# A decay scan moved from TensorE to shifted additions on VectorE, with the shifts done by DMA

## The chip, the cores and the metric

The kernel runs on one core of one Trainium2 chip. The metric is the device time of one execution in microseconds. Before the change the median of three runs is 786.25 us (785.98 to 786.61).

## The reference, cut to what matters

Two blocks work on x of 16 batches x 512 positions x 512 features in float32.

```python
x = x + rmsnorm(layernorm(x), g_res) @ W_in.T + b_in + depool_out   # first block
h_patch = rmsnorm(ctx_2048, g_init)                   # 16 x 512 patches x 1024, the first 512 are used
a = exp(dt * A)                                       # one constant, the same for every row
s[i] = a * s[i-1] + u[i]                              # the scan, over the patches of a batch
depool_out[i] = s[plug[i]]                            # rows picked by a running count of marks
y = layernorm(x)                                      # second block
xr, xk = mixes of y and y moved by one position       # mu_r, mu_k
x = x + sigmoid(xr @ W_r.T) * (relu(xk @ W_k.T)**2 @ W_v.T)
```

The decay `a` is about 0.001, so that after 13 powers nothing is left above the smallest float32 number. For nearly all batches only the first 128 patches are picked; batches with more are called far.

## The kernel before, in words

A batch goes through four stages, and one iteration of the loop works on three batches at once: `b` in the second block, `nxt` = b + 1 in the first block's projection, `new` = b + 2 in its preparation. `batches` (L62) writes iterations -1 and 0 out, runs 1 to 12 as a hardware loop of four rounds of three, and writes the last three out. Every engine has its own instruction list in an order written out by hand, and semaphores hold them together (`reached`, L54, waits for a count that belongs to a batch).

Matrix products are exact to float32 by three products each (`product`, L484 to L486): high by high, high by low, low by high part. ScalarE makes the high part (`copy`, L704), VectorE the low part by subtraction (`low`, L894). TensorE in an iteration: project `nxt` (48 matmuls), gate product of `b` (48), key product (48), value products of tiles 0 and 1 (24), the scan of `new` (3, `scan`, L506), a look at a table whether `new` is far (`far`, L512), value products of tiles 2 and 3 (24), and the transposes of `nxt` (16, `turn`, L578). The scan is a product with a 128 x 128 matrix of the powers of the decay, into bank 3. The fourth group of transposes writes bank 3 too and waits for the semaphores s_copied and far_over of `new` (L584 and L585).

VectorE in an iteration: mixing of `b` with the additions to `nxt` between (L989, L1019), statistics of `nxt` (L1025) and of `new` (L923), normalisation of `nxt` (L1038), four low parts of the keys of `b` (`ka_low`, L894) with two subtractions for xt and the scan's input u (L947) between, u's low part, gating of tiles 0 and 1 (L1044), the scan's output `scanned` (bank 3 plus the bias, L905), the look at the table (L269, L270), far_over, the outputs of tiles 0 and 1 (L919), gating and outputs of tiles 2 and 3.

ScalarE, among the rest, squares ctx, copies xt's high part, squares the keys, copies u's high part, then issues the store of `scanned` to `s_rows` in DRAM (L742), and copies the transposes out (`turned_out`). GpSimd adds rows of `s_rows` to x by four indirect DMAs (L426) once the store has landed. SP waits for these, then loads xt (L285), x (L282) and ctx (L288) of the next `new`, and stores the outputs (L335), all in the order of its list. The lines that fix that order:

```python
rows_added(sp, new.plus(-1))
reached(sp, xt_lo_ready, new.plus(-1), 2, 2); load_xt(new)
reached(sp, out_ready, b.plus(-1), T, T);     load_x(new)
reached(sp, far_over, new.plus(-1), 1, 1);    load_ctx(new)
```

Of the kernel before, what the change touches and what calls it, by code (L numbers as in the profile page):

```python
# [17 lines left out]
P = 128  # L18
# [54 lines left out]

def decay_powers():

    one = np.float32(1.0)
    dt = np.float32(-math.log(-math.expm1(float(np.float32(-EPSILON)))))
    a = np.float32(math.exp(-float(dt)))
    powers = [one]
    while powers[-1] * a > np.finfo(np.float32).tiny:  # L80
        powers.append(powers[-1] * a)
    return [float(p) for p in powers]


def build(nc, x, x_turned, ctx, patch_lens, w_in, b_in, columns, g_init, w_r, w_k, w_v, out):
# [10 lines left out]
    powers = decay_powers()  # L96
    input_gain = math.exp(-EPSILON)

    with ExitStack() as stack:
# [62 lines left out]
        patch_now = sb("patch_now", [P, T], U32)  # L162

# [17 lines left out]
        def f32(ap):  # L181
# [31 lines left out]
            "u_ready u_hi_ready u_lo_ready s_done s_copied s_stored patch_picked")  # L213
        dep_added = [sem(f"dep_added{t}") for t in range(T)]
# [62 lines left out]
        def _(sp):  # L277
# [37 lines left out]

            def iteration(b):
                new = b.plus(2)
                if new.exists(B) and not is_first(new, 1):

                    rows_added(sp, new.plus(-1))  # L320
                    reached(sp, xt_lo_ready, new.plus(-1), 2, 2)
                    load_xt(new)


                    reached(sp, out_ready, b.plus(-1), T, T)
                    if is_first(new, 2):
                        sp.wait_ge(w_lo_ready[WK], C)
                    load_x(new)

                    reached(sp, far_over, new.plus(-1), 1, 1)  # L330
                    load_ctx(new)
                if b.exists(B):
                    for t in range(T):
                        reached(sp, out_ready, b, T, t + 1)
                        sp.dma_start(out_rows[b.number(), :, t, :], gate[:, t, :]).then_inc(stored[t], 16)  # L335
# [145 lines left out]
        def _(pe):  # L481
# [30 lines left out]
            def far(b):  # L512

                n = far_count(pe, b)
                with pe.If(n[0] > 0):
                    for c in range(1, T):
                        done = n[1] * (T - 1) + c
                        if c > 1:
                            pe.wait_ge(far_copied, done - 1)
                        else:  # L520
                            reached(pe, s_copied, b, 1, 1)

                        product(scan_bank(b)[:, :], decay_hi[:, 1, :], decay_lo[:, 1, :], u_hi[:, :], u_lo[:, :],
                                True, False).then_inc(far_carried, 1)
                        pe.wait_ge(far_u_lo, done)
                        product(scan_bank(b)[:, :], decay_hi[:, 0, :], decay_lo[:, 0, :], u_hi[:, :], u_lo[:, :],
                                False, True).then_inc(far_s, 1)
# [50 lines left out]
            def turn(b):  # L578

                for t in range(T):  # L580
                    reached(pe, yn_ready, b, T, t + 1)
                    if b.plus(-1).exists(B):
                        reached(pe, relu_ready, b.plus(-1), C, t + 1)
                    if t == SCAN and b.plus(1).exists(B) and not is_first(b):  # L584
                        reached(pe, s_copied, b.plus(1), 1, 1)  # L585
                        reached(pe, far_over, b.plus(1), 1, 1)
                    for c in range(C):
                        last = nc.tensor.transpose(first_bank(b, t)[:, tile(c)], normed[:, t, c * P:(c + 1) * P],  # L588
                                                   ident[:, :])
                    last.then_inc(yn_turned, 1)  # L590

            def iteration(b):
# [21 lines left out]
                if new.exists(B):  # L614
                    scan(new)
                    far(new)
# [85 lines left out]
        def _(act):  # L702
# [106 lines left out]
            def iteration(b):  # L809
# [18 lines left out]
                if is_first(b):  # L828
                    squares(b)
                    u_high(new)  # L830
# [14 lines left out]
                elif new.exists(B):  # L845
                    if not is_first(b):
                        u_high(new)
# [33 lines left out]
        def _(dve):  # L881
# [61 lines left out]
            def scan_input(b):  # L943

                reached(dve, rs_c_done, b, 1, 1)
                reached(dve, u_lo_ready, b.plus(-1), 1, 1)
                nc.vector.scalar_tensor_tensor(u[:, :], ctx_rows[:, 0:D], rs_c[:, :], g_ctx[:, :],  # L947
                                               ALU.mult, ALU.mult).then_inc(u_ready, 1)

            def far(b):  # L950

                n = far_count(dve, b)
                with dve.If(n[0] > 0):
                    for c in range(1, T):
# [19 lines left out]
                        dve.wait_ge(far_u_hi, done)  # L974
# [76 lines left out]
            def iteration(b):  # L1051
# [32 lines left out]
                if is_first(b):  # L1084

                    ka_low(b, 0)
# [6 lines left out]
                    u_low(new)  # L1093
                    norm_b(nxt)
                    gating(b, 0)
                    gating(b, 1)
                    x_lo(new, 0)
                    x_lo(new, 1)
                    scan_out(new)
                    far(new)  # L1100
                    dve.sem_inc(far_over, 1)
                    add_out(b, 0)
                    add_out(b, 1)
# [5 lines left out]
                if new.exists(B):  # L1109
                    stats_a(new)  # L1110
                    stats_c(new)
                if nxt.exists(B):
                    norm_b(nxt)
                for m in range(C):
                    if b.exists(B):
                        ka_low(b, m)
                    if new.exists(B):
                        if m in (1, 2):
                            x_lo(new, m - 1)
                        if m == 2:  # L1120
                            scan_input(new)
                if is_last(nxt):
                    mixing(nxt, 0, C)
                if new.exists(B):
                    u_low(new)
# [3 lines left out]
                if new.exists(B):  # L1129
                    scan_out(new)  # L1130
                    far(new)
                    dve.sem_inc(far_over, 1)
                if b.exists(B):
                    add_out(b, 0)
                    add_out(b, 1)
# [138 lines left out]
```

## Time and profile before

| | |
|---|---|
| median of three runs | 786.25 us |
| the profiled execution | 788.05 us, its span 786.5 us |
| granted clock of TensorE, mean | 0.986 |
| busy: TensorE, weight loads, VectorE, ScalarE, GpSimd | 756.9, 624.1, 553.8, 413.3, 173.4 us |
| DMA | 85.73 MB, mean 109 GB/s |

A row of a timeline begins with the start in us from the span's start and the duration; a group of like instructions stands on one row. PE is TensorE, DVE VectorE, ACT ScalarE, POOL GpSimd, SP the engine that issues most DMAs; a q behind a name is that engine's own instruction sequencer. The text in square brackets is the idle time of the engine ahead of the row, and what ended it; "issue" is a wait for nothing that the profile shows. Matmuls overlap: they start 0.227 us apart though each lasts 0.39.

### The profile page before, as it was taken

The page shows a single profiled execution, that of the slowest core. Times are in us where ns is not written, and L with a number is a line of the kernel's source. Part 1 is how long each engine was busy: PE and PEld are TensorE (multiplying, and loading weights), DVE is VectorE, ACT ScalarE, POOL GpSimd, SP SyncE. Part 2 cuts the span into 40 slices and gives each one's busy share as a digit, 9 for nine tenths or more (in the row PEclk, how much of TensorE's full clock was granted, in tenths as well). Part 3 has the DMA queues.
Part 4 walks back from the last instruction along what each step waited for, and adds up shares of the span by engine and source line. Part 5 has one row for each costly group of instructions (what it writes and reads, how often), then busy time and mean ns, then how long its engine had stood idle before and what let it go on. Part 6 is the DMA issues. An engine that isn't in the chain of part 4 may idle for free.

```text
span 786.5 us, 11081 instructions
## 1 busy us (share of the span) xinstructions
PE 756.9 (96%) x3462; PEld 624.1 (79%) x3463; DVE 553.8 (70%) x1005; ACT 413.3 (53%) x681; POOL 173.4 (22%) x175
## 2 busy tenths in 40 slices
PE   7669899999999999999999999999999999999997
PEld 4457688888888888888888888888888888888876
DVE  4678797685866868586686858667685867667452
ACT  3317755454654645466464546656454665544760
POOL 7244131311213131121313112131311213130000
PEclk9879999999999999999999999999999999999999
DMA  7476153441706244170624417062441706231011
GB/s 256 150 188 166 60 124 132 112 143 47 209 2 167 88 110 144 46 208 0 156 98 109 144 43 211 0 166 88 108 146 41 212 0 160 94 102 20 1 54 54
DMA packets 42765, 85.73 MB, mean 109 GB/s; under 512 B 3536, under 2 KB 3536, under 8 KB 42704
## 3 DMA queue, kind: packets, MB, share of 16 engines
q1 hardware_dynamic: 30624, 63.71, 21.7%
q0 software_dynamic: 9216, 16.78, 13.5%
q10 hardware_dynamic: 2880, 4.76, 1.7%
q14 instruction: 31, 0.25, 0.1%
q8 instruction: 14, 0.23, 0.1%
HBM read 64.26 MB, written 21.76 MB: 109 GB/s over the span
## 4 chain that ended last, share of the span: by engine, by line
PE 85%; DVE 4%; POOL 4%; issue 2%; ACT 2%; DMA 1%; DVEq 0%; POOLq 0%; ACTq 0%
PE bank L484 27%; PE bank L486 27%; PE bank L485 27%; PE bank L588 3%; POOL ring L426 2%; DMA s_rows<-scanned 1%; POOL decay L363 1%; DVE xk_lo L894 1%; DVE scratch L989 0%; DVE ring L1019 0%; DVE gate L1044 0%; ACT scratch L794 0%; POOL rs_a L389 0%; DVE bn_a L923 0%; DVE bn_b L1025 0%
## 5 line engine op out<-in xcount | busy, mean ns | idle before, releaser
L426 POOL DMA_INDIRECT ring<-s_rows,patch_now x60 | 99.4, 1656 | 245.8 <-DMA s_rows<-scanned 214.6
L894 DVE TENSOR_TENSOR xr_lo<-scratch,xr_hi 128x512 fp32r<-128x512 f32 x124 | 85.6, 690 | 68.9 <-ACT xr_hi L704 68.4
L989 DVE SCALAR_TENSOR_TENSOR scratch<-turned,cols,scratch 128x512 f32<-128x512 f32 x128 | 94.6, 749 | 34.4 <-ACT scratch L749 15.0
L484 PE MATMUL bank<-wi_hi,xt_hi 128*128 128x512 f32 x256 | 104.0, 406 | 5.1 <-DVE xt_lo L894 5.1
L704 ACT ACTIVATE turned<-bank 128x512 f32<-128x512 f32 x64 | 33.4, 604 | 143.3 <-PE bank L588 114.7
L484 PE MATMUL bank<-xk_hi,wk_hi 128*128 128x512 f32 x256 | 99.9, 390 | 2.2 <-DVE xk_lo L894 2.2
L485 PE MATMUL bank<-wi_lo,xt_hi 128*128 128x512 f32 x256 | 101.8, 398 | 0.0
L486 PE MATMUL bank<-wi_hi,xt_lo 128*128 128x512 f32 x256 | 101.5, 396 | 0.0
L484 PE MATMUL bank<-wr_hi,xr_hi 128*128 128x512 f32 x256 | 99.7, 389 | 0.8 <-DVE xr_lo L894 0.8
L486 PE MATMUL bank<-xk_hi,wk_lo 128*128 128x512 f32 x256 | 99.6, 389 | 0.0
L485 PE MATMUL bank<-xk_lo,wk_hi 128*128 128x512 f32 x256 | 99.6, 389 | 0.0
L486 PE MATMUL bank<-wr_hi,xr_lo 128*128 128x512 f32 x256 | 99.6, 389 | 0.0
L485 PE MATMUL bank<-wr_lo,xr_hi 128*128 128x512 f32 x256 | 99.6, 389 | 0.0
L484 PE MATMUL bank<-wv_hi,xr_hi 128*128 128x512 f32 x240 | 94.0, 392 | 2.7 <-DVE xr_lo L894 2.7
L486 PE MATMUL bank<-wv_hi,xr_lo 128*128 128x512 f32 x240 | 93.4, 389 | 0.0
L485 PE MATMUL bank<-wv_lo,xr_hi 128*128 128x512 f32 x240 | 93.4, 389 | 0.0
L749 ACT ACTIVATE scratch<-turned,cols 128x512 f32<-128x512 f32 x128 | 89.5, 711 | 0.5
L704 ACT ACTIVATE xr_hi<-scratch 128x512 fp32r<-128x512 f32 x124 | 77.9, 628 | 20.4 <-DVE scratch L989 17.7
L781 ACT ACTIVATE gate<-bank 128x512 f32<-128x512 f32 x64 | 37.5, 595 | 83.3 <-PE bank L486 83.3
L1044 DVE TENSOR_TENSOR gate<-bank,gate 128x512 f32<-128x512 f32 x64 | 43.6, 688 | 53.2 <-PE bank L486 51.2
L395 POOL TENSOR_TENSOR rs_b<-v_b,half 128x4 f32<-128x4 f32 x16 | 16.5, 1034 | 230.5 <-DVE v_b L1031 230.5
L704 ACT ACTIVATE xk_hi<-scratch 128x512 fp32r<-128x512 f32 x64 | 40.4, 632 | 47.6 <-DVE scratch L989 46.8
(131 smaller groups left out, 1283.5 us busy)
## 6 DMA issues: line engine op xcount, KB each, us to landing
ring<-in_x SPq DMA_DIRECT2D x16, 1024.0 KB, 7.4
out<-gate SPq DMA_DIRECT2D x64, 256.0 KB
xt<-in_x_turned SPq DMA_DIRECT2D x15, 1024.0 KB, 5.2
ctx_rows<-in_ctx SPq DMA_DIRECT2D x16, 512.0 KB, 8.0
s_rows<-scanned ACTq DMA_DIRECT2D x16, 256.0 KB, 2.0
gate<-in_L_xattn_W_in SPq DMA_DIRECT2D x4, 256.0 KB, 3.4
xt<-in_x_turned SPq DMA_DIRECT2D x2, 512.0 KB, 6.3
turned<-in_L_ffn_W_r SPq DMA_DIRECT2D x1, 1024.0 KB, 7.8
```

Source lines behind the costliest of these rows:

```text
L395: nc.gpsimd.tensor_tensor(rs_b[:, :, 0], v_b[:, :, 0], half[:, :], ALU.pow).then_inc(rs_b_done, 1)
L426: pool.indirect_dma_start(ring[b.slot][:, t, :], None, s_rows[:, :], bass.IndirectOffsetOnAxis(ap=rows, axis=0), compute_op=ALU.add).then_ ...
L484: nc.tensor.matmul(where, lhs_hi, rhs_hi, start=start, stop=False)
L485: nc.tensor.matmul(where, lhs_hi, rhs_lo, start=False, stop=False)
L486: return nc.tensor.matmul(where, lhs_lo, rhs_hi, start=False, stop=stop)
L588: last = nc.tensor.transpose(first_bank(b, t)[:, tile(c)], normed[:, t, c * P:(c + 1) * P], ident[:, :])
L704: return nc.scalar.activation(to, of, ACT.Copy)
L749: nc.scalar.activation(scratch[:, i % 2, :], turned[:, c, 0:S], ACT.Copy, scale=cols[:, 3 + which, c:c + 1]).then_inc(carried, 1)
L781: nc.scalar.activation(gate[:, t, :], bank[4 + t][:, :], ACT.Sigmoid).then_inc(gate_ready, 1)
L894: return nc.vector.tensor_tensor(to, whole, high, ALU.subtract)
L989: nc.vector.scalar_tensor_tensor(scratch[:, 2 + i % 2, :], turned[:, c, 1:S + 1], cols[:, 1 + which, c:c + 1], scratch[:, i % 2, :], ALU.m ...
L1044: nc.vector.tensor_tensor(gate[:, t, :], bank[4 + t][:, :], gate[:, t, :], ALU.mult).then_inc(gated, 1)
```

## The change

From batch 2 on there is no scan on TensorE, and no high and low part of u, except in a far batch, where VectorE makes both. Instead VectorE makes four steps `scanned = decay**k * earlier + scanned` with k = 8, 4, 2, 1 (the first adds to u), and ahead of each step SP moves `scanned` (or u) down by k partitions into the new tile `earlier`, by two DMAs: 112 rows, and the rest of 8, 12, 14 or 15. The first rows of `earlier` are zeroed once per batch. After step 3 the bias is added by an instruction of its own. In the loop the input of the scan is made ahead of the low parts of the keys; step 0 takes its place behind the third low part, step 1 follows the fourth, step 2 follows gating 1, and the outputs of tiles 0 and 1 come between steps 2 and 3. The look at the table and far_over follow the bias. TensorE's fourth group of transposes waits for far_over alone. SP loads ctx first, then x, then xt, then issues the shifts, then the output stores. The diff, cut to its core (the semaphore and tile declarations are left out):

```diff
+
+
+def shift_steps(powers):
+
+    return [(k, powers[k] if k < len(powers) else 0.0) for k in (8, 4, 2, 1)]
...
+    steps_of_scan = shift_steps(powers)
+    STEPS, MOST = len(steps_of_scan), P - 16
+    assert len(powers) <= 2 ** STEPS
...
+            def shift_scan(b):
+
+                since = b.plus(-2)
+                for n, (k, _) in enumerate(steps_of_scan):
+                    if n == 0:
+
+                        reached(sp, u_ready, b, 1, 1)
+                    else:
+
+                        reached(sp, earlier_added, since, STEPS, n)
+                    of = scanned if n else u
+                    sp.dma_start(earlier[k:k + MOST, :], of[0:MOST, :]).then_inc(earlier_loaded, 16)
+                    sp.dma_start(earlier[k + MOST:P, :], of[MOST:P - k, :]).then_inc(rest_loaded, 16)
+
             def iteration(b):
                 new = b.plus(2)
                 if new.exists(B) and not is_first(new, 1):
 
+                    reached(sp, far_over, new.plus(-1), 1, 1)
                     rows_added(sp, new.plus(-1))
-                    reached(sp, xt_lo_ready, new.plus(-1), 2, 2)
-                    load_xt(new)
-
+                    load_ctx(new)
 
                     reached(sp, out_ready, b.plus(-1), T, T)
                     if is_first(new, 2):
                         sp.wait_ge(w_lo_ready[WK], C)
                     load_x(new)
 
-                    reached(sp, far_over, new.plus(-1), 1, 1)
-                    load_ctx(new)
+                    reached(sp, xt_lo_ready, new.plus(-1), 2, 2)
+                    load_xt(new)
+                    shift_scan(new)
...
-                            reached(pe, s_copied, b, 1, 1)
+                            if b.fixed and b.number() < 2:
+                                reached(pe, s_copied, b, 1, 1)
+                            pe.wait_ge(far_u_lo, n[1] * T + 1)
 
                         product(scan_bank(b)[:, :], decay_hi[:, 1, :], decay_lo[:, 1, :], u_hi[:, :], u_lo[:, :],
                                 True, False).then_inc(far_carried, 1)
-                        pe.wait_ge(far_u_lo, done)
+                        pe.wait_ge(far_u_lo, n[1] * T + c + 1)
...
                     if t == SCAN and b.plus(1).exists(B) and not is_first(b):
-                        reached(pe, s_copied, b.plus(1), 1, 1)
                         reached(pe, far_over, b.plus(1), 1, 1)
...
                 if new.exists(B):
-                    scan(new)
                     far(new)
...
-                    u_high(new)
...
                 elif new.exists(B):
-                    if not is_first(b):
-                        u_high(new)
                     store_scan(new)
...
                 reached(dve, rs_c_done, b, 1, 1)
-                reached(dve, u_lo_ready, b.plus(-1), 1, 1)
+                if b.fixed and b.number() < 3:
+                    reached(dve, u_lo_ready, b.plus(-1), 1, 1)
+                else:
+
+                    reached(dve, earlier_added, b.plus(-3), STEPS, STEPS)
                 nc.vector.scalar_tensor_tensor(u[:, :], ctx_rows[:, 0:D], rs_c[:, :], g_ctx[:, :],
                                                ALU.mult, ALU.mult).then_inc(u_ready, 1)
 
+            def clear_head(b):
+
+
+                reached(dve, earlier_added, b.plus(-2), STEPS, 0)
+                nc.vector.memset(earlier[0:steps_of_scan[0][0], :], 0.0).then_inc(head_zeroed, 1)
+
+            def scan_step(b, n):
+
+                since = b.plus(-2)
+                reached(dve, earlier_loaded, since, 16 * STEPS, 16 * (n + 1))
+                reached(dve, rest_loaded, since, 16 * STEPS, 16 * (n + 1))
+                if n == 0:
+                    reached(dve, head_zeroed, since, 1, 1)
+
+                    reached(dve, s_stored, b, 16, 0)
+                    reached(dve, u_ready, b, 1, 1)
+                else:
+                    reached(dve, earlier_added, since, STEPS, n)
+                nc.vector.scalar_tensor_tensor(scanned[:, :], earlier[:, :], steps_of_scan[n][1], (scanned if n else u)[:, :],
+                                               ALU.mult, ALU.add).then_inc(earlier_added, 1)
+
+            def add_bias(b):
+
+                reached(dve, earlier_added, b.plus(-2), STEPS, STEPS)
+                nc.vector.tensor_tensor(scanned[:, :], scanned[:, :], bias[:, :], ALU.add).then_inc(s_copied, 1)
...
                 with dve.If(n[0] > 0):
+                    if b.fixed and b.number() < 2:
+
+                        reached(dve, s_done, b, 1, 1)
+                    nc.vector.tensor_copy(u_hi[:, :], u[:, :]).then_inc(far_u_hi, 1)
+                    dve.wait_ge(far_u_hi, n[1] * T + 1)
+                    low(u_lo[:, :], u[:, :], f32(u_hi[:, :])).then_inc(far_u_lo, 1)
+                    dve.wait_ge(far_u_lo, n[1] * T + 1)
...
 
+                    clear_head(new)
                     ka_low(b, 0)
                     stats_c(new)
                     ka_low(b, 1)
@@ -1090,49 +1149,57 @@
                     ka_low(b, 2)
                     stats_a(new)
                     ka_low(b, 3)
-                    u_low(new)
+                    scan_step(new, 0)
                     norm_b(nxt)
                     gating(b, 0)
                     gating(b, 1)
+                    scan_step(new, 1)
                     x_lo(new, 0)
                     x_lo(new, 1)
-                    scan_out(new)
+                    scan_step(new, 2)
+                    add_out(b, 0)
+                    add_out(b, 1)
+                    scan_step(new, 3)
+                    add_bias(new)
                     far(new)
                     dve.sem_inc(far_over, 1)
-                    add_out(b, 0)
-                    add_out(b, 1)
...
                 if new.exists(B):
+                    clear_head(new)
                     stats_a(new)
                     stats_c(new)
                 if nxt.exists(B):
                     norm_b(nxt)
+                if new.exists(B):
+                    scan_input(new)
                 for m in range(C):
                     if b.exists(B):
                         ka_low(b, m)
                     if new.exists(B):
                         if m in (1, 2):
                             x_lo(new, m - 1)
-                        if m == 2:
-                            scan_input(new)
+                        if m in (2, 3):
+                            scan_step(new, m - 2)
                 if is_last(nxt):
                     mixing(nxt, 0, C)
-                if new.exists(B):
-                    u_low(new)
                 if b.exists(B):
                     gating(b, 0)
                     gating(b, 1)
                 if new.exists(B):
-                    scan_out(new)
+                    scan_step(new, 2)
+                if b.exists(B):
+                    add_out(b, 0)
+                    add_out(b, 1)
+                if new.exists(B):
+                    scan_step(new, 3)
+                    add_bias(new)
                     far(new)
                     dve.sem_inc(far_over, 1)
                 if b.exists(B):
-                    add_out(b, 0)
-                    add_out(b, 1)
```

## Rows read from the trace of the kernel before

**Rows 1.** The page's first section: busy time, share of the span, instructions.
```profile
PE 756.9 (96%) x3462; PEld 624.1 (79%) x3463; DVE 553.8 (70%) x1005; ACT 413.3 (53%) x681; POOL 173.4 (22%) x175
```

**Rows 2.** The waits of TensorE's array from 60 us on: total, times, longest.
```profile
PE bank L484 <- DVE xr_lo L894: 3.5, 5, 0.9
PE bank L484 <- DVE xk_lo L894: 2.2, 2, 1.2
```

**Rows 3.** Timeline of TensorE: start, duration, what; one iteration and its ends.
```profile
332.92 1.91 PE L588 MATMUL bank<-ident,normed 128*128 128x128 f32 x16
...
372.76 0.39 PE L484 MATMUL bank<-u_hi,decay_hi 128*128 128x512 f32 x1
...
373.44 0.39 PE L484 MATMUL bank<-wv_hi,xr_hi 128*128 128x512 f32 x1
...
378.89 1.91 PE L588 MATMUL bank<-ident,normed 128*128 128x128 f32 x16
380.55 0.48 PE L484 MATMUL bank<-wi_hi,xt_hi 128*128 128x512 f32 x1
```

**Rows 4.** Timeline of VectorE in the same iteration.
```profile
352.96 0.38 DVE L1029 BATCH_NORM_AGGREGATE mv_b<-bn_b 128x2 f32<-128x6 f32 x4 [0.16 <-DVE bn_b L1025]
...
353.45 2.46 DVE L923 BATCH_NORM_STATS2 bn_a<-ring 128x6 f32<-128x512 f32 x4
...
362.02 0.69 DVE L894 TENSOR_TENSOR xr_lo<-scratch,xr_hi 128x512 fp32r<-128x512 f32 x1 [1.71 <-ACT xr_hi L704]
...
368.51 0.74 DVE L947 SCALAR_TENSOR_TENSOR u<-ctx_rows,rs_c,g_ctx 128x512 f32<-128x512 f32 x1
...
372.28 1.37 DVE L1044 TENSOR_TENSOR gate<-bank,gate 128x512 f32<-128x512 f32 x2 [1.50 <-PE bank L486]
373.74 0.69 DVE L905 TENSOR_TENSOR scanned<-bank,bias 128x512 f32<-128x512 f32 x1
```

**Rows 5.** Wait behind the table look: all, then the last one, outside the loop.
```profile
DVE gate L919 <- issue: 17.0, 13, 1.5
697.00 1.29 DVE L919 TENSOR_TENSOR gate<-gate,ring 128x512 f32<-128x512 f32 x2 [0.89 <-issue]
```

**Rows 6.** The page's DMA issues: KB each, median us from issue to landing.
```profile
ring<-in_x SPq DMA_DIRECT2D x16, 1024.0 KB, 7.4
...
ctx_rows<-in_ctx SPq DMA_DIRECT2D x16, 512.0 KB, 8.0
s_rows<-scanned ACTq DMA_DIRECT2D x16, 256.0 KB, 2.0
gate<-in_L_xattn_W_in SPq DMA_DIRECT2D x4, 256.0 KB, 3.4
```

**Rows 7.** Stretches behind the issue at 374.46; the last columns are DMA share, GB/s.
```profile
375.00:375.30 0.30, 0.30 (x3) 0.23 (x2) 0.00 (x0) 0.00 (x0) 0.00 (x0) 1.00 0.02 7
...
375.90:376.20 0.30, 0.30 (x3) 0.22 (x2) 0.30 (x2) 0.00 (x0) 0.00 (x0) 1.00 0.22 75
```

**Rows 8.** Timelines of ScalarE, GpSimd and SP: issues of DMAs.
```profile
374.46 0.33 ACTq L742 DMA_DIRECT2D s_rows<-scanned  x1
377.27 1.64 POOL L426 DMA_INDIRECT ring<-s_rows,patch_now  x1 [16.84 <-DMA s_rows<-scanned]
343.42 0.41 SPq L285 DMA_DIRECT2D xt<-in_x_turned  x1
```

**Rows 9.** Sequencer of TensorE, L67 (the loop's jump): ns min/median/max, starts.
```profile
L67 PEldq COMPARE_BRANCH  x1: 208/208/208, 378.5 to 378.5; - x1
```

**Rows 10.** Iteration 0: timelines of VectorE and TensorE.
```profile
97.64 1.27 DVE L1044 TENSOR_TENSOR gate<-bank,gate 128x512 f32<-128x512 f32 x2
98.84 2.34 DVE L894 TENSOR_TENSOR xt_lo<-xt,xt_hi 128x1024 fp32r<-128x1024 f32 x2
...
104.73 0.47 PE L484 MATMUL bank<-wi_hi,xt_hi 128*128 128x512 f32 x1
```

**Rows 11.** A stretch of iteration 0: length, PE busy, ..., granted clock, DMA share, GB/s.
```profile
90.00:100.00 10.00, 8.45 (x35) 6.19 (x36) 9.35 (x21) 4.99 (x8) 1.94 (x2) 1.00 0.00 1
```

More of the change, by code:

```diff
@@ L162, in build @@
         patch_now = sb("patch_now", [P, T], U32)
+        earlier = sb("earlier", [P, D])
         def part(row, start, shape, dt):
@@ L213, in build @@
             "u_ready u_hi_ready u_lo_ready s_done s_copied s_stored patch_picked")
+        head_zeroed, earlier_loaded, rest_loaded, earlier_added = sems("head_zeroed earlier_loaded rest_loaded earlier_added")
         dep_added = [sem(f"dep_added{t}") for t in range(T)]
@@ L973, in far @@
                         nc.vector.tensor_copy(u_hi[:, :], u[:, :]).then_inc(far_u_hi, 1)
-                        dve.wait_ge(far_u_hi, done)
+                        dve.wait_ge(far_u_hi, n[1] * T + c + 1)
                         low(u_lo[:, :], u[:, :], f32(u_hi[:, :])).then_inc(far_u_lo, 1)
```

## The prediction

> **What bounds the kernel now.** I read the page's first section, the waits of TensorE, then the timelines of TensorE and VectorE over one round of the loop. TensorE is busy 96% of the span [rows 1]. After 60 us its array waits seven times for anything, 5.7 us in all [rows 2], so its own work is the bound. One iteration (one batch through the stages) lasts 45.97 us, from the transposes at 332.92 to those at 378.89 [rows 3]. The three matmuls of the scan stand at 372.76, and the next product follows at 373.44: they cost 0.68 us of a full array [rows 3]. VectorE has holes: 1.71 us before the first low part of the keys, 1.50 us before the gating, and another behind the scan's output [rows 4, 5].
>
> **What the change takes from TensorE.** Batches 2 to 15 lose their scan: 14 x 0.68 = 9.5 us if nothing else moves. ScalarE loses a copy, VectorE a subtraction and the read of the bank.
>
> **What it adds: a chain of four steps.** Step 0 of VectorE takes the place that the input of the scan had, at 368.51 for 0.74 us [rows 4]. The input moves into the 1.71 us hole ahead of 362.02, behind the statistics of 353.45 and the normalisation; its first shift then has some 7 us, more than it needs. The 8-row memset is small and ahead of a wait too. From step 0 on each step needs the one before it moved through a DMA pair issued by SP, and nothing hides that. Let G be the time from the end of one step to the start of the next. No row shows a transfer from SBUF to SBUF, so I bound it:
> - Nearest row: the 256 KB store of the scan, from SBUF, lands 2.0 us after its issue [rows 6]. Issued at 374.46, its packets run from about 375.3 to 376.1 [rows 7, 8]: 0.84 us before the first, some 0.75 of moving, some 0.4 to the landing. 112 of 128 rows save 1/8 of the moving: 1.9.
> - The second transfer is issued 0.4 us behind the first (0.33 us an issue on ACT [rows 8], and a gap). Its one row per engine stands behind seven of the first; it lands at about 2.0.
> - Waking SP costs 0.03 (store issued at 374.46, addition ended at 374.43 [rows 4, 8]); two further waits and their register operations in front of the next step cost about 0.1.
>
> So G is 1.9 at the least; at most it is that of the 256 KB loads from DRAM, 3.4 us and 0.2 [rows 6]. I take 2.15, near the store, which also reads SBUF.
>
> Then, in the frame of [rows 4]:
> - step 0: 368.51 to 369.26. The last low part of the keys, right behind it, keeps its place.
> - step 1: 371.41 to 372.16. Gating 0 and 1 keep theirs (372.28, for 1.37).
> - step 2: 374.31 to 375.06; two output additions fit behind it.
> - step 3: 377.21 to 377.96.
> - bias: from 378.12 (a dependent instruction starts 0.16 later [rows 4]), 4.4 us after the old scan output at 373.74.
> - far_over: behind that output comes the look at the table of far batches. Its mean gap is 17.0/13 = 1.31 us [rows 5], and with 0.69 for the addition 2.00 from its start; the increment is some 0.12 before the next instruction. So far_over rises at 380.00.
>
> **Who waits for that.** The fourth group of transposes waits for far_over (L578 to 586), unchanged in the code; before, the rise at about 375.4 was 4.8 us early. The sixteen take 1.66 us, 378.89 to 380.55 [rows 3], so without the scan the fourth group would start at 378.21 + 1.25 = 379.46. It now waits to 380.00, 0.54 us. And TensorE's sequencer, ahead of the array until now, stands at that wait. Behind it come the wait itself (0.08), eight instructions (0.25), every third iteration the loop's jump (0.208 and its registers, 0.43 in all, 0.14 on average [rows 9]) and 0.40 of waits and registers up to the projection's first matmul (in the timeline of the sequencer from 380.2, the matmul at 380.55 [rows 3]): 0.87; the small terms are estimates from instructions of 20 to 50 ns around [rows 9]. The projection starts at 380.87 where it started at 380.55. An iteration is longer by 0.32 us, not shorter by 0.68. In formula: 3G - 6.13.
>
> **The sum.** Twelve iterations of the loop: 12 x 0.32 = +3.8. The last with a scan stands outside the loop: its look takes 0.89 + 0.69 = 1.58 instead of 2.00 [rows 5] and there is no jump: 0.32 - 0.56 = -0.2. Iteration 0 is different: there VectorE works without holes and its sequencer had the look done in advance. Step 0 is over before 96, and the gatings, 97.64 to 98.9, come before step 1 (98.9 to 99.6), two subtractions (2.34 us [rows 10]) before step 2, at 101.85 to 102.5; step 3 starts at 104.65 and ends at 105.4, the bias starts at 105.55, far_over rises 1.47 later at 107.0, and the projection starts at about 107.95 where it started at 104.73 [rows 10]: +3.2. Together +6.9 on the profiled execution's 788.05, so 794.9. That execution is 1.8 above the median of the runs; against 786.25 the forecast is 793.1.
>
> **What stays covered.** The bias comes 4.1 us later relative to the next projection (378.12 - 380.87 against 373.74 - 380.55), and so do the store, the indirect additions (POOL at 377.27 [rows 8]) and the loads that wait for them (343.42 becomes 347.5). x is now second, behind ctx of half its size. Before it stood behind xt and landed 0.5 + 7.4 = 7.9 us after the first issue [rows 6]; 1.3 less is 6.6, at 354.1. The statistics of 353.45 slip by 0.65 into the hole ahead of 358. xt, last, lands at about 356.6 (before, the last of the three landed 8.0 us after its own issue [rows 6], 1.1 behind the first), and ScalarE reads it from 358.2. The indirect additions had landed by 343.4, when SP issued; 4.1 us later each is still ahead of the addition that reads it, the second by only 0.3. SP's output stores stand behind the shifts, whose last is issued at 375.1, ahead of the first output. The clock was 1.00, the 2.4 GHz level, also where the array was busy 8.45 of 10 us [rows 11]; waits of half a microsecond don't touch it.
>
> The Trainium skill, SBUF — State Buffer, section The DMA setup-cost knee, says that every transfer pays a roughly fixed 2 us beside its bytes. With the 0.6 us of moving in these rows a shift would land after 2.6 and G would be about 2.7. The store of 256 KB lands after 2.0 in all, moving included [rows 6], so this trace disagrees for that transfer; no row settles it for SBUF to SBUF.
>
> **Rivals.** The time moves by 41 us per microsecond of G (12 x 3, 3 and 2 in the two iterations outside), so no change lies at G = 1.98.
> - Hidden (faster): the shift lands before 1.95, since an SBUF target might confirm sooner than DRAM. From G = 1.82 down the fourth group waits no longer in the loop: 13 x -0.68 + 2.6 for iteration 0 = -6.2, about 780. For it: only 0.17 us separate me from no change. Against it: 0.84 before the first packet is on the sending side, and two issues in a row add to it.
> - Slow shifts: at 2.7, because seven rows an engine run unevenly, or the confirmation is slow: 0.55 x 41 = +22.5 on my forecast, 815. For it: loads of the same size took 3.4, and 2.7 is a third of the way from my value to the upper bound.
>   The Trainium skill's fixed 2 us (the section above) would give about this G.
> - The late loads: if the indirect additions slow down beside the later stores so that x comes 3 us later still, the hole ahead of 362.02 is used up and the low parts that TensorE needs come about 1 us late, 13 x 1 = +13: 806. Against it: the margins above.
> - The change doesn't take TensorE's work away: not so by the diff; the scan call is gone from the iteration.
>
> **Chances.** Forecast (G 2.02 to 2.4): 0.53, by itself 787.8 to 803.5. At or about no change (G 1.94 to 2.02): 0.13. Hidden or partly hidden: 0.22. Slow shifts 0.08. Late loads 0.04. This gives faster 0.22, within 0.2% (1.6 us, about what can be told from no change) 0.13, slower 0.65. The range, G 1.87 to 2.45: 782 to 805.
>
> **What would show it.** Three scan matmuls fewer per batch, and TensorE with a new wait for VectorE or for nothing named ahead of a transpose or of a projection, some 0.5 to 1 us each iteration; an iteration of 46.3 us; idle time of VectorE ahead of steps 1, 2 and 3, of 1.2, 0.7 and 0.9 us, ended by a DMA from `scanned`; a landing of about 2.0 us for `earlier<-scanned`; iteration 0 longer by 3 us. It is wrong if the landing is under 1.8 us, if the fourth group of transposes starts without a gap, or if new waits stand at the low parts of the keys.

## The result and the profile after

The changed kernel took 827.31 us (median of 4 runs, 826.14 to 831.60); the kernel before took 786.43 us beside it (4 runs, 785.98 to 786.74). The ratio is 1.053, interval 1.049 to 1.057: slower by 5.3%. The forecast was 793.1 with a range of 782 to 805. The sign was right, the size was not, and the range missed by 22 us. The profiled execution took 831.60 us (span 830.0), 43.6 more than the profiled execution before.

The page's first section of the changed kernel answers to [rows 1]:

```profile
PE 764.9 (92%) x3420; PEld 626.6 (75%) x3421; DVE 586.5 (71%) x1061; ACT 406.9 (49%) x667; POOL 189.1 (23%) x175
```

There are 42 matmuls fewer, 14 x 3, so the work left TensorE as planned. Its busy time nevertheless grew by 8 us and its share fell from 96% to 92%. The waits of TensorE's array from 60 us on answer to [rows 2] (total, times, longest):

```profile
PE bank L613 <- DVEq L1201: 32.5, 13, 3.0
PE bank L613 <- DVEq L1165: 4.3, 1, 4.3
PE bank L508 <- DVE xr_lo L915: 2.7, 4, 0.8
PE bank L508 <- DVE xk_lo L915: 2.2, 2, 1.2
```

The last two were there before. The first two are new: the fourth group of transposes (L613) waits for far_over, which VectorE's sequencer raises, 36.8 us in 14 batches. One row of the page's groups, and three of its DMA issues, name what VectorE itself waits for:

```profile
L993 DVE SCALAR_TENSOR_TENSOR scanned<-earlier,scanned 128x512 f32<-128x512 f32 x42 | 29.1, 692 | 76.0 <-DMA earlier<-scanned 76.0
...
earlier<-scanned SPq DMA_DIRECT2D x42, 224.0 KB, 2.7
...
s_rows<-scanned ACTq DMA_DIRECT2D x16, 256.0 KB, 2.0
earlier<-u SPq DMA_DIRECT2D x14, 224.0 KB, 2.7
```

The 42 dependent steps idle 1.8 us each for a transfer that lands 2.7 us after its issue. Here is one iteration; the timeline of VectorE, with the square brackets giving the idle time ahead of a row, answers to [rows 4]:

```profile
392.50 0.68 DVE L993 SCALAR_TENSOR_TENSOR scanned<-earlier,u 128x512 f32<-128x512 f32 x1
393.48 0.69 DVE L915 TENSOR_TENSOR xr_lo<-scratch,xr_hi 128x512 fp32r<-128x512 f32 x1 [0.29 <-ACT xr_hi L728]
396.04 0.69 DVE L993 SCALAR_TENSOR_TENSOR scanned<-earlier,scanned 128x512 f32<-128x512 f32 x1 [1.86 <-DMA earlier<-scanned]
396.65 1.28 DVE L1102 TENSOR_TENSOR gate<-bank,gate 128x512 f32<-128x512 f32 x2
399.62 0.69 DVE L993 SCALAR_TENSOR_TENSOR scanned<-earlier,scanned 128x512 f32<-128x512 f32 x1 [1.69 <-DMA earlier<-scanned]
400.23 1.29 DVE L940 TENSOR_TENSOR gate<-gate,ring 128x512 f32<-128x512 f32 x2
403.21 0.69 DVE L993 SCALAR_TENSOR_TENSOR scanned<-earlier,scanned 128x512 f32<-128x512 f32 x1 [1.69 <-DMA earlier<-scanned]
403.94 0.69 DVE L999 TENSOR_TENSOR scanned<-scanned,bias 128x512 f32<-128x512 f32 x1
406.11 1.29 DVE L1102 TENSOR_TENSOR gate<-bank,gate 128x512 f32<-128x512 f32 x2 [1.48 <-issue]
```

From the end of one step to the start of the next, G, it is 2.86, 2.89 and 2.90 us (396.04 less 392.50 and 0.68, and so on). The order of the rows is the one forecast; the gaps aren't. The issues of the second shift, in the timeline of SP, and the end of the iteration on TensorE, which answers to [rows 3]:

```profile
393.22 0.53 SPq L337 DMA_DIRECT2D earlier<-scanned  x1
393.79 0.77 SPq L338 DMA_DIRECT2D earlier<-scanned  x1
```

```profile
402.20 1.47 PE L613 MATMUL bank<-ident,normed 128*128 128x128 f32 x12
406.00 1.11 PE L613 MATMUL bank<-ident,normed 128*128 128x128 f32 x4 [2.32 <-DVEq L1201]
406.76 0.77 PE L508 MATMUL bank<-wi_hi,xt_hi 128*128 128x512 f32 x1
407.33 0.63 PE L509 MATMUL bank<-wi_lo,xt_hi 128*128 128x512 f32 x1
```

TensorE finishes twelve transposes, stops 2.32 us, does four, and then its matmuls start 0.43 us apart, not 0.227. The granted clock in the next view says why: the first line is the stretch behind the stop, the second all of the run behind 72 us, and the second fence the same of the kernel before. The columns are the stretch, its length, the busy time of PE, PEld, DVE, ACT and POOL, the granted clock, the DMA share and GB/s:

```profile
406.00:409.00 3.00, 3.00 (x9) 2.56 (x10) 2.49 (x4) 2.57 (x5) 1.53 (x1) 0.50 0.07 27
72.00:830.00 758.00, 712.57 (x3184) 587.04 (x3182) 540.30 (x964) 379.72 (x621) 153.56 (x113) 0.98 0.40 114
```

```profile
72.00:786.00 714.00, 705.14 (x3226) 584.75 (x3224) 507.65 (x908) 386.21 (x635) 137.09 (x113) 1.00 0.34 101
```

Behind the stop TensorE runs at 0.50 of its clock, the 1.2 GHz level, and over all of the run behind 72 us the mean is 0.98; before, it was 1.00. The clock fell behind six of the fourteen stops (those of 4.3, 3.0, 2.9, 3.0, 2.3 and 3.0 us), each time for 3.4 or 6.8 us. It didn't fall behind any of the last six, from 500 us on, though they were of 2.0 to 3.0 us too. What tells the one kind from the other wasn't found.

### The profile page after: what moved, and what is told of

Same layout as the page of the kernel before. It is cut to its first block, busy times and chain, and to the rows that moved or that the text cites. A ratio compares the mean times of both kernels' runs of the same rounds, so it can differ in the third digit from the quotient of the medians.

```text
span 830.0 us, 11255 instructions
## 1 busy us (share of the span) xinstructions
PE 764.9 (92%) x3420; PEld 626.6 (75%) x3421; DVE 586.5 (71%) x1061; ACT 406.9 (49%) x667; POOL 189.1 (23%) x175
## 4 chain that ended last, share of the span: by engine, by line
PE 57%; DMA 15%; DVE 11%; ACT 5%; issue 5%; POOL 4%; DVEq 2%; SPq 1%; POOLq 0%; ACTq 0%
PE bank L508 19%; PE bank L509 19%; PE bank L510 19%; DMA earlier<-scanned 13%; DVE scanned L993 5%; DVE xt_lo L915 2%; POOL ring L450 2%; DMA s_rows<-scanned 2%; ACT scratch L818 1%; PE bank L613 1%; POOL decay L387 1%; ACT scratch L816 1%; ACT xr_hi L728 1%; DVEq L280 1%; SPq L337 1%
## 5 line engine op out<-in xcount | busy, mean ns | idle before, releaser
L450 POOL DMA_INDIRECT ring<-s_rows,patch_now x60 | 110.2, 1837 | 332.3 <-DMA s_rows<-scanned 294.3
L508 PE MATMUL bank<-wi_hi,xt_hi 128*128 128x512 f32 x256 | 108.9, 425 | 5.4 <-DVE xt_lo L915 5.4
L509 PE MATMUL bank<-wi_lo,xt_hi 128*128 128x512 f32 x256 | 106.2, 415 | 0.0
L510 PE MATMUL bank<-wi_hi,xt_lo 128*128 128x512 f32 x256 | 105.7, 413 | 0.0
L993 DVE SCALAR_TENSOR_TENSOR scanned<-earlier,scanned 128x512 f32<-128x512 f32 x42 | 29.1, 692 | 76.0 <-DMA earlier<-scanned 76.0
L613 PE MATMUL bank<-ident,normed 128*128 128x128 f32 x256 | 36.9, 292 | 43.0 <-DVEq L1201 32.5
L613 PEld LDWEIGHTS bank<-ident,normed 128*128 128x128 f32 x256 | 31.1, 150 | 48.6 <-DVEq L1201 32.7
```

The costliest lines, as they stand in the source:

```text
L450: pool.indirect_dma_start(ring[b.slot][:, t, :], None, s_rows[:, :], bass.IndirectOffsetOnAxis(ap=rows, axis=0), compute_op=ALU.add).then_ ...
L508: nc.tensor.matmul(where, lhs_hi, rhs_hi, start=start, stop=False)
L509: nc.tensor.matmul(where, lhs_hi, rhs_lo, start=False, stop=False)
L510: return nc.tensor.matmul(where, lhs_lo, rhs_hi, start=False, stop=stop)
L993: nc.vector.scalar_tensor_tensor(scanned[:, :], earlier[:, :], steps_of_scan[n][1], (scanned if n else u)[:, :], ALU.mult, ALU.add).then_i ...
```

## The experiments

The kernel before, run beside all of these, took 786.5 to 787.2 us. What the runs had to decide: is the loss the chain of dependent shifts (theory), or the other things that the change touches; what sets G; what the clock costs; and which waits tie the chain to TensorE.

**One transfer instead of four.**

```diff
 in shift_scan, for n in 0..3:
-    of = scanned if n else u
-    (both transfers)
+    if n == 0: (both transfers, from u)
 in scan_step:
-    wait for the transfers of step n
+    wait for the transfers of step 0
```

> Leaves out the transfers of steps 1 to 3 (every step adds the first shift again; the scan's numbers are wrong), all four additions, the bias and the order stay. Theory A (the chain of transfers holds TensorE back): without the three gaps the bias starts about 400.3 in the frame where it started at 403.9, far_over rises before the fourth group is due, the period falls to 45.3 us, and the time to 777 to 780. Rival B (VectorE's added work, SP's new order or the late loads cost it): 800 or more. Rival C (half of the loss is the clock for a cause of its own): about 790.

Measured: 781.28 us, ratio 0.992 (0.990 to 0.995), within 2 us of the theory. From one first transpose to the next it takes 45.29 us in twelve of the iterations: 45.97 less exactly the 0.68 us of the scan's three products. Everything else of the change is in this kernel (four additions, the moved input, the memset, the new order of loads, one shift a batch), and all of it is hidden in the loop. The exception is iteration 0, where one period is 49.41: VectorE comes late there by its own work, and TensorE still stops 2.3 us for far_over. The whole loss against the kernel before goes with the three dependent transfers.

**What a shift costs: its shape and its number.**

```diff
 e2_112_alone
-    earlier[k+112:128] <- of[112:128-k]
 e4_112_in_place
-    (both transfers)
+    earlier[16:128] <- of[16:128]
 e3_128_in_place
-    (both transfers)
+    earlier[0:128] <- of[0:128]
```

> Leaves out the second transfer of each shift (the last rows of the moved tile stay old). If the 112-row transfer sets the gap: it still lands after 2.7 us, the gap is 2.75 instead of 2.88, time 820 to 824. If the second transfer and its issue set it: the gap falls to 2.2, time below 800.

> Each shift is one transfer of rows 16 to 127 to the same rows: 112 rows, not moved. If the count of 112 makes it slow: issue 0.53, landing 2.6 to 2.7, time 815 to 822, as with 112 rows moved. If the move to other partitions makes it slow: landing 2.0, time 784 to 790.

> Each shift is one transfer of all 128 rows to the same rows, so nothing is shifted. If a transfer within SBUF costs what the store did and only the shape of this one is dear: issue 0.33, landing 2.0, gap 2.15, the wait of the fourth group some 0.1 to 0.2 us, time 784 to 790, about the forecast. If the target SBUF is slower by itself: landing 2.7, time 820 to 824.

Measured: 812.78 (ratio 1.032, 1.027 to 1.038), 811.35 (1.031, 1.028 to 1.034) and 802.71 us (1.020, 1.016 to 1.024). The views of all instructions that touch `earlier` give the durations of the issue (ns, min/median/max) and the landings. First the changed kernel, then e2_112_alone, then e3_128_in_place:

```profile
L337 SPq DMA_DIRECT2D earlier<-scanned x42: 517/532/551, 96.0 to 740.0; - x42
L338 SPq DMA_DIRECT2D earlier<-scanned x42: 766/818/1252, 96.5 to 740.5; - x42
...
DMA to landing us min/median/max: 2.6/2.7/3.3
```

```profile
L337 SPq DMA_DIRECT2D earlier<-scanned x42: 511/512/517, 94.8 to 719.7; - x42
...
  DMA earlier<-scanned: 63.8, 41
...
DMA to landing us min/median/max: 2.6/2.6/3.1
```

```profile
L337 SPq DMA_DIRECT2D earlier<-scanned x42: 464/465/471, 94.3 to 710.4; - x42
...
  DMA earlier<-scanned: 52.5, 40
...
DMA to landing us min/median/max: 2.3/2.3/3.8
```

The median G of the 42 gaps is 2.89 in the changed kernel, 2.69 without the short transfer, 2.66 with 112 rows that are copied onto their own rows, 2.36 with 128 rows. So the displacement of the rows costs 0.03 at most; the short transfer costs 0.20; and 112 rows cost 0.3 more than 128, though they are fewer bytes. The packets in the traces say where the 0.3 lies (medians): the first starts 1.13 us behind the issue with 128 rows and 1.18 with 112, they run for 0.79 and 1.07 us, and from the end of the last to the landing it takes 0.39 and 0.36. In one transfer of 112 rows that I counted through, six packets or fewer are in flight in the last 0.3 us, where 16 are before. Why they are spread so isn't shown. Each of the three lies between the two results that I had set against each other. None makes the loss vanish: at the 2.36 of one full transfer the kernel is still 2% slower. The wait of TensorE's array for far_over falls with G as it should, from 36.8 us in all to 25.1, 24.4 and 16.1.

**The clock by itself.**

```diff
 in the turn of the fourth group, ahead of the wait for far_over:
+    for _ in range(10): matmul into the free bank, result not used
```

> The changed kernel with ten more products on TensorE (results not used) into a bank that is free, placed right ahead of the fourth group of transposes, so that the array works on through most of its stop for far_over. The chain of shifts and additions is untouched, so far_over comes no earlier. Theory A (TensorE's array idles 2.3 to 4.5 us there, the granted clock falls to 1.2 GHz for a stretch of 3.4 us behind it in 7 to 9 of 14 iterations, and these stretches cost some 10 us in all): no half-speed stretch after the first 72 us of the span, granted clock back at 0.983 or more, periods of 47.5 to 48.0 us (48.6 where an instruction fetch delays a shift) instead of 49.4 to 51.3, about 814 to 818 us. Rival B (the clock's fall has another cause, or costs nothing because VectorE's and ScalarE's work sets the pace behind it): 826 us or more.

Measured: 819.91 us (ratio 1.042, 1.040 to 1.045), 7.4 less than the changed kernel, with ten products more a batch. The stretch behind 72 us in this kernel:

```profile
72.00:817.00 745.00, 731.08 (x3316) 602.08 (x3314) 539.25 (x962) 378.99 (x621) 151.34 (x113) 1.00 0.41 116
```

Behind iteration 0 the periods are 47.6 to 48.6 us where five of the changed kernel's were 49.4 to 51.3. One stretch at half clock was left against my expectation, at 108.1 us, behind the 2.2 us that remained of iteration 0's stop. The idle array costs twice: for the stop itself, and for the half clock behind it. The second part is 7.4 us of the medians. The result lies 2 us above what I expected, where I had priced the half clock at some 10 us in all: too much by a quarter.

**Which waits tie the chain to TensorE.**

```diff
 e6_over_early, VectorE
+    far(new); far_over        ahead of scan step 1
-    far(new); far_over        behind the bias
 e7_store_on_sp
-    ScalarE: store_scan(new)  ahead of turned_out
+    SP: the same store, behind the fourth shift
 e8_both
     both edits
```

> The changed kernel with far (the sum of the middle entries, with the look at the register and far_over behind it) moved ahead of the scan's first addition on VectorE, so that far_over doesn't wait for the four additions. Theory A (two things hang on the chain's end: far_over, and behind it ScalarE, which issues the store of the scanned rows and only then turns the transposed rows; the store waits for the bias addition): TensorE stops for ScalarE's turned rows almost as long as it did for far_over, about 822 to 828 us. Rival B (only far_over holds TensorE): the scan is hidden, 776 to 782 us.

> The changed kernel with the store of the scanned rows issued by SyncE behind the shifts, not by ScalarE; far_over stays behind the four additions. Theory A (far_over binds by itself, ScalarE's part lies just behind it): 822 to 828 us, no gain. Rival B (only ScalarE's wait at the store holds the work up): 776 to 782 us.

> Both edits together: far ahead of the scan on VectorE, and the store of the scanned rows issued by SyncE. Theory A (far_over and the store are the only two that hang on the chain within the stretch that bounds): the chain of four shifts runs beside TensorE's other work, TensorE's stop is gone, no half-speed stretch behind it, periods near 45.3 us (46.0 less the 0.68 us of the scan's products), 776 to 783 us, faster than the kernel before. Rival B (a third thing hangs on it: VectorE's additions of the scan come between the normed rows and their turned copies, or the loads issued behind the shifts, or the indirect additions that wait for the store, come late and stop TensorE elsewhere): 790 to 815 us.

Measured: 821.82 (ratio 1.045, 1.043 to 1.047), 829.40 (1.054, 1.052 to 1.057) and 788.56 us (1.002, 1.001 to 1.004). The waits of TensorE's array from 60 us on, in e6_over_early, then in e7_store_on_sp:

```profile
PE bank L508 <- ACT turned L728: 34.9, 14, 4.8
```

```profile
PE bank L616 <- DVEq L1202: 32.7, 13, 3.2
PE bank L616 <- DVEq L1166: 4.8, 1, 4.8
```

Each edit alone removes one of two waits that end almost together (undisturbed periods are 47.4 us in e6_over_early and 47.5 in e7_store_on_sp and the changed kernel), and the other takes over whole: 34.9 us for the turned rows of ScalarE, which stands at its issue of the scan's store until the bias is added, or 37.5 for far_over. Only together do they set TensorE free of the chain. Theory A of both held to within 1.4 us, but e8_both did not reach its 776 to 783, nor quite its rival's 790 to 815. Behind iteration 0 its periods are 45.3 to 47.7 us. Three views of it show what comes late next: the waits of all engines, those of TensorE's array from 60 us on, and the timeline of SP:

```profile
ACT xt_hi L731 <- DMA xt<-in_x_turned: 30.1, 14, 4.1
```

```profile
PE bank L511 <- DVE xr_lo L916: 6.6, 11, 0.8
```

```profile
351.36 0.38 SPq L295 DMA_DIRECT2D xt<-in_x_turned  x1
```

xt is issued 18.7 us behind the first transposes (332.70 in this iteration); before it was 10.5 [rows 3, 8]. The store of the scan still comes at the end of the chain, the indirect additions behind the store, and SP's loads wait for these.

> The kernel of e8_both (far ahead of the scan, the store of the scanned rows by SyncE) with one more edit: SyncE issues ctx and xt ahead of its wait for the added rows, not behind it; only x stays behind that wait. In e8_both xt was issued 19 us after the first group of transposes (before: 10.5 us) and ScalarE's conversion of it started 2.5 to 2.8 us later than before, while some periods were 46.1 to 47.7 us instead of 45.3. Theory A (the late xt is what kept e8_both from its gain): conversions back at 25.3 us, all periods 45.3 us, 777 to 783 us. Rival B (VectorE's order, with far ahead and three additions of the chain held by transfers, makes the low parts late): no change from e8_both, 785 to 791 us.

```diff
 SP, in iteration:
     wait far_over; load_ctx(new)
+    wait xt_lo_ready; load_xt(new)
     rows_added(new.plus(-1)); ... load_x(new)
-    wait xt_lo_ready; load_xt(new)
```

Measured: 797.31 us (ratio 1.014, 1.011 to 1.016), worse than e8_both. ScalarE's conversion came 25.3 to 26.0 us behind the first transposes in all but one iteration of the loop (before 25.3, in e8_both 26.0 to 29.7), nearly as theory A has it, but VectorE now waited for the indirect additions (first fence, the waits of all engines), and TensorE more for the low parts (second, its array from 60 us on):

```profile
DVE ring L1077 <- DMA ring<-s_rows,patch_now: 41.2, 22, 4.2
```

```profile
PE bank L510 <- DVE xr_lo L915: 13.1, 19, 1.5
```

In e8_both VectorE's wait was 7.6 us, 9 times, and TensorE's 6.6, 11 times. The 1 MB of xt now moves while the additions do, and these are slower or later; how much of that is contention was not separated. My theory was wrong here, and so was its rival, which forecast no change. That the late xt is what kept e8_both from its gain is therefore read from the traces and not shown: the one run that took the lateness away brought another wait.

**A shorter chain.**

```diff
 def shift_steps(powers):
-    for k in (8, 4, 2, 1)
+    for k in (2, 1)             e10_two_steps
+    for k in (4, 2, 1)          e11_three_steps
 VectorE: the calls of scan_step for the steps that are gone
```

> The changed kernel with two steps of the scan instead of four (shifts by 2 and 1; what the shifts by 8 and 4 add carries factors of the decay's eighth and fourth power, 1e-24 and 1e-12, under the rounding of float32). Two gaps of 2.88 us and two additions of 0.69 us leave the chain: 7.1 us, more than TensorE's stop of 2.3 to 3.3 us. Theory A (the chain's length against the room of about 6.65 us is all that matters): no stop at far_over, no half-speed stretch, each of 14 periods shorter by the 0.68 us of TensorE's products, 776 to 781 us, faster than before. Rival B (the order of SyncE's loads or the wait of SyncE within the chain makes something else late): 784 to 792 us, as with e8_both.

> The changed kernel with three steps of the scan (shifts by 4, 2 and 1), the third addition in the place of the fourth. The chain is shorter by one gap and one addition, 3.57 us, where TensorE's stop costs 2.2 us in most periods and 3.3 us in those in which an instruction fetch delays a shift. Theory A (threshold: two gaps fit, three don't): periods of 45.3 us but for the first (47 to 48), 779 to 784 us. Rival B (the cost falls in proportion to the number of transfers: two thirds of what four steps cost over e1_first_shift_only): 810 to 814 us.

Measured: 779.05 us with two steps (ratio 0.990, 0.988 to 0.992) and 784.53 with three (0.997, 0.996 to 0.998); both are faster than before. In e10_two_steps, the timeline of VectorE, then of TensorE:

```profile
364.12 0.68 DVE L992 SCALAR_TENSOR_TENSOR scanned<-earlier,u 128x512 f32<-128x512 f32 x1
...
367.73 0.69 DVE L992 SCALAR_TENSOR_TENSOR scanned<-earlier,scanned 128x512 f32<-128x512 f32 x1 [1.95 <-DMA earlier<-scanned]
...
370.74 0.68 DVE L998 TENSOR_TENSOR scanned<-scanned,bias 128x512 f32<-128x512 f32 x1
```

```profile
373.82 1.91 PE L612 MATMUL bank<-ident,normed 128*128 128x128 f32 x16
375.48 0.48 PE L507 MATMUL bank<-wi_hi,xt_hi 128*128 128x512 f32 x1
```

The gap is as long as ever (2.93 here, 2.98 in the median), but there is only one, and it fits into the room ahead of the fourth group; the sixteen transposes are one group again and the period is 45.3 us from iteration 1 on. With three steps the periods are 45.3 to 46.6, and 47.4 in iteration 0. The loss is a threshold, not a price per transfer: two thirds of the loss was the rival's forecast (810 to 814).

## Why the prediction was wrong, step by step

- **Taken from TensorE, 14 x 0.68: right.** e1_first_shift_only shows the period of 45.29.
- **What was costed at nothing on VectorE and SP: right in the loop.** The moved input, the memset, ctx ahead of x and xt, and the wait for the added rows cost nothing in e1_first_shift_only behind iteration 0. In the changed kernel VectorE waits 6.8 us in all for x, and TensorE's waits for low parts are no more than before.
- **G: wrong, and the step that failed.** I read 1.9 for the transfer out of the store of 256 KB and 2.15 for G. The median is 2.89, the mean over the 42 gaps 3.01. The bounds (1.9 to 3.6) held it, but the nearest row was not near: each term was too small but the last. The first packet starts 1.19 us behind the issue, not 0.84; the packets of 112 rows run for 1.1 us, not 7/8 of 0.75 (e2_112_alone); the second transfer adds 0.20, not 0.1. From the last packet to the landing it is 0.36, near the 0.4 that I took. With the formula's own 41 us per microsecond, 0.86 of mean is 35 us.
- **The frame around the chain: right in kind, some 0.65 us too long.** From step 3 to the bias it takes 0.73, not 0.91; far_over rises 1.63 to 1.98 behind the bias (mean 1.75), not 1.88; and the restart behind it, forecast at 0.87 with its share of the loop's jump, is 0.48 without the jump and some 0.2 more with it: the group starts 0.07 behind far_over and the projection 0.41 behind the group. With 2.88 for G this gives 3 x 2.88 - 6.13 - 0.18 - 0.25 - 0.39 = +1.69 for a look of 1.63 and no jump; the trace has 47.53 less 45.97, +1.56. Over the twelve iterations of the loop this took back some 8 us.
- **Iteration 0 and the last: right in working.** In the forecast's own frame, from one projection's start to the next, iteration 0 gained 4.4 us (109.14 for 104.73) where +3.2 was forecast. Two of its gaps hang on G, as the forecast had it, and 0.73 more in each of them makes 4.7. The last gained 2.2 for -0.2, of which 2.6 by its gaps of 2.85, 3.36 and 2.87, less the frame.
- **The clock: a term put at nothing, and the second step that failed.** "Waits of half a microsecond don't touch it" is borne out by e3_128_in_place, where nine stops of 0.4 to 0.8 us behind 256 us left the clock at 1.00. But it didn't answer the question. With the true G the stops were 2.0 to 4.3 us, and the clock fell behind six of the fourteen. That is 7.4 us of the median. Of the profiled execution it is some 10 us: the twelve iterations of the loop took 36.9 us more than before in the changed kernel and 26.9 more in e5_filled. (The two profiled executions differ by 12.5 us, but 1.8 of that lie ahead of 57 us, where no chain has begun.) A term that is zero at one value of G isn't zero at the end of the range; the price of 41 us per microsecond left it out.
- **The sum with what was measured:** 6.9 + 35 (G) - 8 (frame) + 10 (clock) = 44, against 43.6 in the profiled execution.
- **Rivals.** "Slow shifts" was what happened, with 0.08 of the chances, and for one of its two reasons: the rows of a transfer of 112 do run unevenly, while the confirmation isn't slow (0.36). Its G of 2.7 is the landing time itself, and its 815 is what the shape without the short transfer gave (812.78). "Hidden" failed on the chip, and "Late loads" stayed covered. The price of G was right to within the frame: e3_128_in_place against the changed kernel moves 24.6 us for 0.52 of mean G, of which 0.52 x 41 = 21; the clock fell less often there too, behind two stops.

The forecast's other weakness was in the width: a quantity without a row, counted three times in series in each of 14 batches, was given 0.3 to either side.

## What to carry to other kernels

A transfer in a chain of dependent steps costs its whole time from issue to landing. Before such a chain is given in exchange for 0.68 us of a busy engine, look at what room it has (here some 6.5 us for three gaps: three of 8.65 in all, in the iteration that ends at 358 us, brought the fourth group 2.1 us late) and count a gap at some 2.9 us. Shorten the chain before moving its ends, for everything that hangs on its end has to move with it: here two waits, each hiding the other, and a store with the loads behind it. And price a stop of the array with its after-effect: of fourteen stops of 2.0 to 4.3 us here, six were followed by 3.4 or 6.8 us at half clock.

## What the runs showed of the hardware that I had not expected

- A transfer of 112 rows from SBUF to SBUF lands later (2.6 us) than one of 128 rows (2.3), and its issue takes 0.51 against 0.465 us; in place or displaced makes a difference of 0.03 at most. The issue of the short one takes 0.82 with 12 to 15 rows and 0.72 with 8.
- The same 256 KB land in 2.0 us in DRAM (the store) and in 2.3 in SBUF. The Trainium skill, DMA: Bandwidth & Descriptors, section Latency and other measured facts, holds that the receipt from the target memory dominates the fixed cost and that HBM is the slowest target; these two rows stand against it. The issuing engine isn't the reason: in e7_store_on_sp, where SP issues the store, it lands in 2.0 too. Nor is the receipt: from the end of the last packet to the landing it is 0.35 us in DRAM and 0.39 in SBUF, and the rest of the difference lies ahead of the first packet (0.84 against 1.13 behind the issue). The Trainium skill, SBUF — State Buffer, section The DMA setup-cost knee, advises 128 partitions for transfers that bound the time; the rows agree, by 0.3 us.
- The first gap of the changed kernel's loop is 3.86 to 3.91 us in every third iteration, at least 0.95 longer. In the trace an 8 KB packet of the instruction queue stands in one DMA engine at 296.8, and the shift's last landing is at 298.19, 0.9 behind the one before it. The cause is read from the trace alone; no run took the fetch away. This stretch is around it, and then the addition that waited:

```profile
q14 instruction: 1, 0.01, 0.4%
```

```profile
298.26 0.69 DVE L993 SCALAR_TENSOR_TENSOR scanned<-earlier,scanned 128x512 f32<-128x512 f32 x1 [2.88 <-DMA earlier<-scanned]
```

- The restart behind a wait is short. In the iteration from 460 us TensorE's sequencer does nothing from 500.6 on, far_over rises at 505.21, the group starts at 505.28 and the projection at 505.70. The sequencer did stand at the wait, as forecast: the loop's jump comes 0.1 us behind the group's start (553.16 for 553.06) where before it came 1.65 us ahead of it. But with no jump to make, what it then has to do is hidden beside the group's own 0.41 us.
